# Three gates through the exponential and VectorE's reciprocal, with a new order of the first and late calls, in a decoder layer on one core

## The reference

```python
# 1 self attention, sigmoid weights
qn, kn = layer_norm(x @ Wq.T + bq), layer_norm(x @ Wk.T + bk)
attn = sigmoid(qn @ kn.T / 16 - log(1024))
x = layernorm(x + ((attn @ v) @ Wo.T + bo) * layerscale)
# 2 cross attention over 77 keys, 16 heads of 16, softmax weights
x = layernorm(x + cross_attention(ctx, ctx, x))
# 3 time mix
x_prev = x shifted by one row
xr, xk = mu_r * x + (1 - mu_r) * x_prev, mu_k * x + (1 - mu_k) * x_prev
r = sigmoid(xr @ W_r)
out = r * (square(relu(xk @ W_k)) @ W_v)
x = layernorm(x + out)
```

## Time and profile before

| | us |
|---|---|
| median of 3 runs | 538.51 (538.36 to 538.99) |
| profiled execution, its time | 538.83 |
| its span | 537.0 |
| TensorE busy | 515.7 |
| ScalarE busy | 453.6 |
| VectorE busy | 442.9 |
| GpSimd busy | 380.5 |
| table loads on ScalarE | 61, 78.3 us in all |

### The profile page before, as it was taken

One profiled execution on the slowest core, in us unless ns is written; L12 is line 12 of the kernel. 1 busy time (PEld: TensorE's weight loads), 2 busy tenths in 40 slices (PEclk: granted clock), 3 DMA queues, 4 the chain that ended last, 5 costly groups with the idle time before them and its releaser, 6 DMA issues.

```text
span 537.0 us, 12711 instructions
## 1 busy us (share of the span) xinstructions
PE 515.7 (96%) x4530; PEld 469.5 (87%) x4530; DVE 442.9 (82%) x994; ACT 453.6 (84%) x1135; POOL 380.5 (71%) x554
## 2 busy tenths in 40 slices
PE   9999999999999999999999999999999877999994
PEld 5788989898989898989898989989888757999994
DVE  4797859878887979797988888778878878899996
ACT  3665479998989898989898988899989888898974
POOL 1774747676867676675758584967868888779986
PEclk9999999999999999999999999999999998999999
DMA  6410120110111020201010101030501000011112
GB/s 191 133 42 22 37 59 8 39 39 3 26 37 40 21 59 4 59 3 60 2 40 2 40 2 40 2 100 3 197 1 40 1 2 1 2 41 60 60 60 99
DMA packets 23252, 22.50 MB, mean 42 GB/s; under 512 B 1707, under 2 KB 23187, under 8 KB 23188
## 3 DMA queue, kind: packets, MB, share of 16 engines
q1 hardware_dynamic: 22754, 21.35, 12.6%
q10 hardware_dynamic: 434, 0.34, 0.2%
HBM read 14.55 MB, written 6.82 MB: 40 GB/s over the span
## 4 chain that ended last, share of the span: by engine, by line
PE 78%; ACT 12%; DVE 5%; issue 2%; POOL 1%; DMA 1%; POOLq 0%; DVEq 0%; SPq 0%; ACTq 0%
PE st L289 19%; PE acc L289 16%; PE xb L289 12%; PE proj L289 9%; PE xb L2063 6%; PE xb L2047 6%; ACT p_sb L580 4%; PE xb L2034 4%; PE proj L1943 2%; ACT L531 2%; PE xb L1855 2%; ACT carry L468 1%; DVE xm L1457 1%; DMA wraw<-in_wkT 1%; PE xb L1993 1%
## 5 line engine op out<-in xcount | busy, mean ns | idle before, releaser
L580 ACT ACTIVATE p_sb<-xb,neg_mx 128x77 f32<-128x77 f32 x512 | 119.3, 367 | 5.2 <-DVE neg_mx L1392 5.0
L1031 POOL TENSOR_TENSOR fold<-p_sb 128x640 f32<-128x640 f32 x32 | 50.6, 1581 | 77.8 <-ACT p_sb L580 77.8
L1036 POOL TENSOR_TENSOR p_sb<-p_sb,rc 128x1280 f32<-128x1280 f32 x32 | 75.2, 2351 | 25.5 <-DVE rc L1405 25.4
L531 ACT ACT_TABLE_LOAD x61 | 78.3, 1283 | 1.1
L289 PE MATMUL acc<-vv_hi,aT_hi 128*128 128x256 f32 x256 | 76.3, 298 | 0.0
L289 PE MATMUL st<-qkT_hi 128*128 128x256 f32 x256 | 75.0, 293 | 0.3 <-ACT a_sb L539 0.3
L289 PE MATMUL st<-qkT_lo,qkT_hi 128*128 128x256 f32 x256 | 72.4, 283 | 0.0
L289 PE MATMUL st<-qkT_hi,qkT_lo 128*128 128x256 f32 x256 | 72.3, 283 | 0.0
L289 PE MATMUL acc<-vv_lo,aT_hi 128*128 128x256 f32 x256 | 72.2, 282 | 0.0
L289 PE MATMUL acc<-vv_hi,aT_lo 128*128 128x256 f32 x256 | 72.2, 282 | 0.0
L1392 DVE TENSOR_REDUCE neg_mx<-xb 128x4 f32<-128x308 f32 x128 | 53.6, 468 | 18.1 <-PE xb L2034 18.1
(11 more groups left out here) (247 smaller groups left out, 1708.2 us busy)
## 6 DMA issues: line engine op xcount, KB each, us to landing
xraw<-in_xT SPq DMA_DIRECT2D x16, 256.0 KB, 3.2
xs<-in_x SPq DMA_DIRECT2D x16, 256.0 KB, 3.4
out_y<-y SPq DMA_DIRECT2D x16, 256.0 KB, 2.1
x_kept<-xs SPq DMA_DIRECT2D x10, 256.0 KB, 2.2
x2s_a<-x_kept SPq DMA_DIRECT2D x2, 512.0 KB, 5.3
x2s_b<-x_kept SPq DMA_DIRECT2D x2, 512.0 KB, 6.7
x2s_c<-x_kept SPq DMA_DIRECT2D x1, 512.0 KB, 3.7
cT<-in_cT SPq DMA_DIRECT2D x1, 308.0 KB, 3.1
```

Source lines behind the costliest of these rows:

```text
L531: act.activation(spare[:, n:n + 1], nlogs[:], func)
L580: ex = act.activation(weights(t)[:, h // KH * (H // 2) + KH * n + h % KH, 0:SC], logits[n][:, h * SC:(h + 1) * SC], ACT.Exp, bias=neg_mx[: ...
L1031: pool.tensor_tensor(fold[:].rearrange("p (h k) -> p h k", k=FO), p[:, :, 0:FO], p[:, :, FO:2 * FO], ALU.add).then_inc(fo_pool.sem, 1)
L1036: pool.tensor_tensor(weights(t), weights(t), rc[:, t % 2].rearrange("p (h o) -> p h o", o=1) .to_broadcast([P, H, SP]), ALU.mult).then_inc ...
```

## The change

The gates of pairs 0, 1 and 2 no longer come from the sigmoid. ScalarE computes exp(-a) (`gate_exp`), and VectorE bounds it at 1e38, adds 1 and takes the reciprocal (`gate_open`), which is the sigmoid of a. `gated` of these pairs waits for VectorE's own semaphore `go_dve`. Pairs 3 to 15 keep the sigmoid.

```diff
+NG = 3
+                def gate_exp(i):
+                    table_for(ACT.Exp)
+                    w.wait_ge(*fr_pe.at(i))
+                    act.activation(gate[:, i % 3], fr_bank(i), ACT.Exp, scale=-1.0).then_inc(fr_act.sem, 1)
...
+                def gate_open(i):
+                    w.wait_ge(*fr_act.at(i))
+                    g = gate[:, i % 3]
+                    dve.tensor_scalar(g, g, 1e38, 1.0, op0=ALU.min, op1=ALU.add).then_inc(go_dve.sem, 1)
+                    w.wait_ge(*go_dve.at(i, 1))
+                    dve.reciprocal(g, g).then_inc(go_dve.sem, 1)
...
                 def gated(i):
                     w.wait_ge(*fv_pe.at(i))
-                    w.wait_ge(*fr_act.at(i))
+                    w.wait_ge(*(go_dve.at(i) if i < NG else fr_act.at(i)))
...
                     elif i >= 4:
-                        w.wait_ge(*qk_dve.at(i - 2))
+                        w.wait_ge(*qk_dve.at(i - 4 if i < 6 else i - 2))
...
                 first_qk()
                 on_all_rows(0)
                 qk(2)
+                on_all_rows(1)
                 qk(3)
-                on_all_rows(1)
                 qk(4)
...
                 weights_t(27, 0)
-                attend(63)
+                x2(1)
                 weights_t(27, 1)
                 weights_t(27, 2)
+                attend(63)
                 mixed(13)
...
                 attended(15)
-                mixes(1)
                 stats1(15)
                 mixed_lo(13)
```

More of the change, by code:

```diff
@@ L691, in _ @@
                 w.wait_ge(*consts_pool.at(0))
-                copy(spare[:, 8 * NSPARE - 1:], nlogs[:])
+                act.activation(spare[:, 8 * NSPARE - 1:], nlogs[:], ACT.Identity)
                 act.dma_start(columns[:], io["columns"]).then_inc(load_id.sem, 16)
@@ L1549, in mix_round @@
                 def mix_round(i):
-                    at(stats3, i - 11, NJ, 10)
-                    at(key_squares_lo, i - 8, NJ, 11)
-                    at(mixes, i - 5, NJ, 12)
-                    at(mix_lo, i - 6, NJ, 16)
-                    at(gated, i - 9, NJ, 16)
+                    at(gated, i - 10, NJ, 7)
+                    at(mixes, i - 6, NJ, 11)
+                    at(mix_lo, i - 7, NJ, 22)
+                    at(key_squares_lo, i - 9, NJ, 12)
+                    at(stats3, i - 11, NJ, 8)
                 dve.memset(a_sb[:, 0, 0:D], 0.0).then_inc(zeros_dve.sem, 1)
@@ L1564, in _ @@
                 qk_bias(0)
+                bv_wide()
+                qk_bias(1)
                 qk_stats(0)
-                qk_bias(1)
                 qk_stats(1)
                 qk_bias(2)
-                bv_wide()
                 qk_stats(2)
@@ L1752, in _ @@
                 mixed_lo(14)
-                gated(0)
+                stats2(13)
                 maxima(31, 0)
@@ L1779, in _ @@
                 stats3(1)
+                mixes(6)
                 mix_lo(5)
-                mixes(6)
                 gated(3)
                 stats3(2)
+                mixed_lo(15)
                 mixes(7)
+                mix_lo(6)
                 key_squares_lo(4)
                 stats3(3)
-                mix_lo(6)
-                mixed_lo(15)
+                mix_lo(7)
                 mixes(8)
-                mix_lo(7)
                 gated(4)
+                crossed(15)
                 key_squares_lo(5)
-                crossed(15)
                 mixes(9)
@@ L2164, in mix_round @@
                 def mix_round(i):
-                    at(x2, i - 1, NJ, 17)
-                    at(mix_values, i - 6, NJ, 11)
-                    at(mix_keys, i - 5, NJ, 12)
-                    at(receptance, i - 4, NJ, 18)
+                    at(receptance, i - 4, NJ, 13)
+                    at(mix_values, i - 5, NJ, 12)
+                    at(x2, i, NJ, 15)
+                    at(mix_keys, i - 3, NJ, 13)
                 warm_up()
@@ L2370, in _ @@
                 mix_keys(4)
+                receptance(4)
                 x2(8)
-                receptance(4)
                 receptance(5)
+                mix_keys(5)
+                dense(15)
                 x2(9)
-                mix_keys(5)
+                mix_values(4)
                 mix_keys(6)
-                mix_values(4)
-                dense(15)
+                x2(10)
                 receptance(6)
-                x2(10)
                 mix_values(5)
```

482 lines of the change are left out of this document (242 added, 240 removed).

## The result

The changed kernel is slower: 551.01 us (median of 4 runs, 549.64 to 553.01) against 538.43 us (537.74 to 538.99) on the same chip, a ratio of 1.0229 (95% interval 1.020 to 1.0259). Forecast were 542.4 us, in a range from 534.8 to 546: the sign was right, the size was not. The profiled execution is the longest of the four, 553.01 us with a span of 551.2, so the 14.2 us that its trace shows as loss are 1.6 more than the 12.6 between the medians.

The account below looks back on a forecast made before the run. TensorE, busy 515.7 of 537.0 us, was taken as the bound, with VectorE full beside it late. TensorE's lag of 3.7 us less 1.1 won back plus 1.3 of clock made +3.9 on 538.51: 542.4 us, range 534.8 to 546.

Parts of the forecast that it names:

- the sign: Whole kernel: slower than before, given a chance of 0.60, with 0.31 for faster and 0.09 for the same.
- The start: First calls before the rounds: an earlier `qk(4)`, partly held by a late `tqk(0)`, gains 0.65 us.
- The wait at `qk(4)`: At the start, TensorE's 0.72 us wait at 14.53 goes, as `qk(4)` waits for an earlier bias add.
- The reciprocal: VectorE's gates of pairs 0 to 2: 6.3 ns for an element, 3.35 us for each 128x512.
- Rivals A: VectorE's reciprocal is cheap, 0.68 us each with a fixed extra: 535.4 us, faster; chance 0.28.
- rival B: VectorE's reciprocal takes eight steps for each element, 4.4 us: 545.6 us; chance 0.12.
- The walk over VectorE: VectorE from `cross_scores(31)` on, call by call: `mixes(5)` 6.9 us later, at 470.9, `mix_values(2)` 6.1 later, at 469.8.
- the product of pair 1: VectorE's `y<-acc,gate` of pair 1 ends TensorE's longest wait, with a clock near one half behind it.
- The late order before 440: TensorE around tiles 27 to 29: the new order brings `cross_scores(29)` some 1.3 us forward, bounds 0 and 3.9.
- The slack: From 460 to 520 us idle time wins back at most 3.2 us on VectorE and 1.1 on TensorE.
- 1.3 of clock: TensorE, idle before `mix_values(2)`, loses its clock again: 1.3 us counted of 1.7.
- Rival C: Slow reciprocals paid for by the front's whole 4.55 us, held clock and slack: 538.5 us, no change; chance 0.12.

Follow-up runs that it names:

- e4: The changed kernel with the first calls of all four engines in the order of before, late calls as changed: 545.62 us, ratio 1.0118.
- g2: The kernel before with only the shorter wait of `qk(4)`, on the next bias add but one behind the earlier limit: 538.78 us, ratio 1.0005.
- e1: The changed kernel with the ScalarE exchange undone, `xt_hi(1)` again ahead of `qk_biases`: 548.41 us, ratio 1.0173.
- h3: The changed kernel with the ScalarE exchange undone and VectorE's first statistics and bias adds ordered as before: 546.66 us, ratio 1.0143.
- f1: The changed kernel with all first lists of before and the three reciprocals over 16 of 512 columns, output not the reference's: 536.08 us, ratio 0.9941.
- g3: The changed kernel with first lists of before, gate 0's reciprocal whole, those of gates 1 and 2 over 16 columns: 540.27 us, ratio 1.0028.
- e3: The changed kernel with each of the three reciprocals over 16 of 512 columns, output not the reference's: 542.15 us, ratio 1.0053.
- e2: The kernel before with only the ScalarE exchange made, `qk_biases` ahead of `xt_hi(1)`: 542.64 us, ratio 1.0047.
- f4: The kernel before with the first calls of after on all four engines and nothing else of the change: 543.89 us, ratio 1.0092.
- h1: The changed kernel with first lists of ScalarE, GpSimd and VectorE as before, only TensorE's new one kept: 547.22 us, ratio 1.0154.
- h2: The changed kernel with the ScalarE exchange undone and TensorE's first list as before, the others' new lists kept: 555.59 us, ratio 1.0305.
- f3: The changed kernel with first lists of before and every gate as tanh(a/2) on ScalarE, no reciprocals for gates: 535.68 us, ratio 0.9935.

## Why the prediction was wrong

*The start, the step that failed.* "I take 0.65 us" of gain; it lost 5.4 us by medians of the runs (551.0 against e4's 545.6), and 7.95 in the profiled execution. `qk(4)` was to start by 13.5 and started at 19.41. I priced the two edits that I had looked for. The wait at `qk(4)` is worth nothing in time (g2): the next step was not ready. I noted that `bv_wide` and `qk_bias(1)` now delay the first statistics, and counted this as hidden; it cost 1.8 us at `mixed(0)` (105.00 in e1, 103.18 in h3). And I did not see the exchange of `qk_biases` and `xt_hi(1)` on ScalarE, two lines that stand in the diff: 3.0 us by the runs, 5.2 at `mixed(1)` in the profiled execution (e1). The wait is 2.02 of them, and 9.26 us at half the clock are worth up to 4.6 more; the sum is over 5.2 because without them e1 waits 1.11 us for the late `qk_sb` at `tqk(0)`. The trace of before has the rows for it, `bqk` at 9.83 and the copy at 6.93.

*The reciprocal.* Right, 3.353 us for 3.35, and so close by luck: starts are read to 0.01 us, so the 0.10 us of which the cost by element was made leaves at least 0.3 us either way. 16, 256 and 512 columns took 0.25, 1.753 and 3.353 us, a line of 6.25 ns for an element. Rivals A (cheap) and B (4.4 us) are out. The Trainium skill, "VectorE: DVE Perf Modes", section "First, the fixed hardware budget", says that a reciprocal is an iterative divide with a repeat count of 8. Read as eight steps of a plain operation for each element, that gives the estimate of 4.4 us in rival B. The traces agree that an element takes several steps, but not with eight: 6.25 ns against 1.04 to 1.2 ns of a plain operation (0.53 or 0.60 us over 512) are five to six.

*The walk over VectorE.* Shifted by the 7.29 us by which `mixed(14)` was late, it holds. The first gate opening was to end at 452.2 (it ended at 452.1), the small reciprocal of tile 31 at 453.9 (453.9), the third opening at 469.1 (469.3), `mix_values(2)` to start at 469.8 (469.9); `mixes(5)` came at 472.0 instead of 470.9, since one of the two low parts ahead of it took 1.78 us instead of 0.68 (below). VectorE in order of time, after, with the 7.29 us in:
```profile
456.07 3.35 DVE L1489 RECIPROCAL gate<-gate 128x512 f32<-128x512 f32 x1
459.53 0.69 DVE L1496 TENSOR_TENSOR y<-acc,gate 128x512 f32<-128x512 f32 x1
460.14 0.81 DVE L1405 TENSOR_REDUCE sm<-fold 128x16 f32<-128x640 f32 x1
460.98 0.25 DVE L1412 RECIPROCAL rc<-sm 128x16 f32<-128x16 f32 x1
...
467.55 0.69 DVE L1419 COPY pT<-xb 128x512 f32<-128x512 f32 x1 [0.35 <-PE xb L2065]
...
468.61 3.35 DVE L1489 RECIPROCAL gate<-gate 128x512 f32<-128x512 f32 x1
...
473.20 3.35 DVE L1489 RECIPROCAL gate<-gate 128x512 f32<-128x512 f32 x1
476.47 0.63 DVE L1496 TENSOR_TENSOR y<-acc,gate 128x512 f32<-128x512 f32 x1
477.01 2.38 DVE L1290 TENSOR_TENSOR xmT_lo<-xm,xmT_hi 128x512 fp32r<-128x512 f32 x2
479.31 1.65 DVE L1464 SCALAR_TENSOR_TENSOR xm<-xb,mu,carry 128x256 f32<-128x256 f32 x4
```
That VectorE has no pause worth the name from 450 on is as foretold; that the product of pair 1 would end TensorE's longest wait is not. The longest is behind the first reciprocal, through `sums(31)` and GpSimd's scaling, 4.0 us: I had that path in the walk ("2.2 us later") and did not follow it to TensorE. There are two late stretches at a lowered clock, not one, as these windows of after show (3.9 us at 0.64, 3.6 at 0.73):
```profile
463.90:467.80 3.90, 3.89 (x23) 3.89 (x24) 3.55 (x11) 1.07 (x2) 3.75 (x7) 0.64 0.00 0
...
477.00:480.60 3.60, 3.45 (x32) 2.36 (x36) 3.60 (x7) 1.05 (x3) 2.26 (x2) 0.73 0.00 0
```

*The late order before 440.* -1.3 was -0.66 here and -0.79 in e4 (its 439.80 against 440.26, with `mixed(0)` 0.33 later): the right sign, half the size. *The slack.* From `mixed(14)` on I had +5.9 (5.7, less 1.1 won back, plus 1.3 of clock); it was +6.91. Whether something was won back and something else lost beside it, the runs do not part: f1 to e4 is 9.5 us for 9.3 of work, and g3 splits it unevenly. Put together, -0.65 - 1.3 + 5.9 = +3.9 stood against +7.95 - 0.66 + 6.91 = +14.2, and 8.6 of the 10.3 us between them is the start. By medians it is 0.65 + 5.4 = 6.1 of the 8.6 us between 542.4 and 551.0. Rival C ("paid for") is out with the slack. For a kernel with the first lists of before the same sum, without its start term, gives 543.0; e4 took 545.6, 2.6 us more, and this rest lies in the late part.

What stays open: why the half clock of the start lasted 9 us in one profiled execution, some 7 in another (e3) and some 3.4 in two (e2, f4) with the same wait; which calls brought the 2.8 us between e1 and e4 beyond the 1.8 of the first statistics; and whether the low part of 2.8 us alone brings the 1.2 us between `mixed(0)` and `mixed(1)`. h1, with TensorE's new list and the others' old ones, does not have them (25.9), and h2, with TensorE's old one and the others' new ones, has them (27.1), so they come with the lists of ScalarE, VectorE or GpSimd.

## What to carry to other kernels

A diff of an order is read in full where an engine is still filling: for each exchanged pair ask what the one moved ahead waits for, and who stands behind it. Here two exchanged lines cost some 3 us (5.2 in the profiled execution), with no instruction added. A divide over whole tiles on an engine that has work queued behind it was paid in full in sum, 9.5 us for 9.3; a function of the table that is already loaded (tanh for the sigmoid) took the load away and put nothing in its place. And an order and the edit that it was made for are measured together: late order alone +0.45%, tanh alone -0.16%, both -0.65%.

## What the runs showed of the hardware

- RECIPROCAL on VectorE costs by element, 6.25 ns (128x16 0.25, 128x256 1.753, 128x512 3.353 us), five times a plain operation of the 512-column shape. Over all runs one size differs by 3 ns at most (3.352 to 3.355 us).
- Behind a wait of 2.02 us at the start TensorE's clock was at half for 9.3 us in the profiled execution of after. In others with the same wait it was shorter; by windows of 2 us as above, e2 is back at 1.00 by 16 us, f4 too, e3 by 20 us. These kernels spread by 2.7 to 4.4 us from run to run (after 549.6 to 553.0, e2 539.7 to 544.1), but a spread is no sign of this wait: before, which does not have it, has 537.4 to 541.5 in 21 runs, and f3 0.7 us in five.
- Tanh ran behind the exponential without a table load of its own: 58 loads, three fewer than before, and those of the earlier trace rows are gone.
- A low part of `xm` on VectorE took 1.78 us (two in 2.38, the row at 477.01) where its median is 0.684. GpSimd's sum of `y` and `x2` ran beside it:
```profile
477.18 1.66 POOL L1090 TENSOR_TENSOR y<-y,x2s_a 128x512 f32<-128x512 f32 x1 [5.75 <-DVE y L1496]
```
- This is no single case. In the 17 traces 119 of 1496 low parts of `a` and `xm` take over 1.3 us, up to 2.8, and every one of them ends 0.545 to 0.555 us behind the end of a GpSimd TENSOR_TENSOR that ran beside it (here 479.39 behind 478.84). They read two tiles in SBUF. `kkT_lo` and the product into `y`, which read one of their two from a PSUM bank, took 0.693 us at most in 544 cases. That reads as the low part standing until GpSimd is done; no run moves one of the two alone. A new order of calls changes which of them meet: here it adds 6.2 us to VectorE's busy time.
